# A dense layer's second product written token-major, its outputs rearranged by way of HBM

## The reference

```python
x = x + conv3x3(_gn(x), L0)                  # 8 -> 8 channels, bias
x = x + conv3x3(_gn(x), L1)
x = x + dense(_gn(x))                        # below
x = x + conv3x3(_gn(x), L3)

# dense: one expert e per channel; each image row n is a token of d = 256
h   = einsum('bend,edf->benf', x, w1) + b1   # f = 1024
h   = gelu(h)
out = einsum('benf,efd->bend', h, w2) + b2
```

## Time and profile before

| | |
|---|---|
| median of three runs | 575.45 us |
| the profiled execution | 576.91 us |
| its span | 575.1 us |
| mean granted TensorE clock | 0.971 |
| TensorE busy | 520.0 us, 90% |
| VectorE busy | 374.1 us, 65% |
| ScalarE busy | 291.8 us, 51% |
| GpSimd busy | 159.1 us, 28% |

### The profile page before, as it was taken

How to read it: one execution, slowest core, us unless ns; L and a number is a source line. 1 busy time by engine, 2 the same in 40 slices (tenths; PEclk the granted TensorE clock), 3 DMA queues, 4 the chain that set the end, 5 groups by cost and what they waited for, 6 DMA issues and landing times.

```text
span 575.1 us, 9042 instructions
## 1 busy us (share of the span) xinstructions
PE 520.0 (90%) x3326; PEld 255.5 (44%) x3326; DVE 374.1 (65%) x644; ACT 291.8 (51%) x354; POOL 159.1 (28%) x181
## 2 busy tenths in 40 slices
PE   0879999896979999999999999999999989978990
PEld 0534445364544444444444444444444545445440
DVE  4969999888766395194293392481547598678541
ACT  2599988333635453353362361461444828766510
POOL 4679888853270000000000000000000001677610
PEclk9889999898899999999999999999999999989996
DMA  8845555533020122022011112102123300134769
GB/s 327 324 111 146 150 132 139 143 101 147 0 75 1 73 74 74 0 73 73 0 73 73 31 42 73 73 0 73 74 74 108 112 0 2 45 81 107 242 200 349
DMA packets 14168, 57.41 MB, mean 100 GB/s; under 512 B 3116, under 2 KB 3244, under 8 KB 11052
## 3 DMA queue, kind: packets, MB, share of 16 engines
q1 hardware_dynamic: 11820, 49.30, 26.9%
q10 hardware_dynamic: 2316, 7.68, 3.7%
HBM read 30.03 MB, written 8.39 MB: 67 GB/s over the span
## 4 chain that ended last, share of the span: by engine, by line
PE 62%; DVE 19%; ACT 5%; POOL 4%; DMA 3%; issue 2%; ACTq 1%; SPq 1%; POOLq 0%; DVEq 0%
PE PS L1007 28%; PE PS L978 27%; DVE X L665 6%; DVE ST L626 6%; PE PS L878 2%; POOL XN L360 2%; ACT XN L439 2%; PE PS L952 2%; DMA X<-x 2%; PE PS L936 2%; PE PS L885 1%; DVE X L681 1%; ACT SCR L444 1%; DVE XT L674 1%; DVE SM L641 1%
## 5 line engine op out<-in xcount | busy, mean ns | idle before, releaser
L978 PE MATMUL PS<-XT,W1S 128*128 (+1 forms) x768 | 172.0, 383 | 1.7 <-DVE XT L674 1.7
L1007 PE MATMUL PS<-HID,W2S 128*128 128x512 f16 x768 | 170.8, 379 | 1.6 <-DVE W2S L688 1.6
L476 ACT ACTIVATE SCR<-PS,CONST 128x512 f32<-128x512 f32 x128 | 87.0, 686 | 64.4 <-PE PS L978 27.8
L978 PEld LDWEIGHTS PS<-XT,W1S 128*128 128x128 f16 x768 | 75.6, 99 | 91.1 <-issue 4.7
L1007 PEld LDWEIGHTS PS<-HID,W2S 128*128 128x128 f16 x768 | 75.1, 98 | 87.5 <-issue 1.8
L360 POOL TENSOR_TENSOR XN<-SCR,XN 128x1024 f16<-128x1024 f32 (+1 forms) x61 | 100.4, 1670 | 26.5 <-ACT SCR L444 26.5
L688 DVE SCALAR_TENSOR_TENSOR W2S<-W2F,W2S 128x2048 f16<-128x2048 f32 x10 | 22.9, 2291 | 114.6 <-ACT W2S L472 114.6
L333 POOL MEMSET HALO<- 48x520 f16 x12 | 6.3, 526 | 316.8 <-PE PS L978 316.3
L626 DVE BATCH_NORM_STATS2 ST<-X 128x6 f32<-128x512 f32 x128 | 81.5, 681 | 9.4 <-DMA X<-x 8.2
L439 ACT ACTIVATE XN<-X,SC 128x1024 f16<-128x1024 f32 (+1 forms) x61 | 64.1, 1050 | 33.9 <-POOL SC L351 27.6
L665 DVE SCALAR_TENSOR_TENSOR X<-PS,X 128x512 f32<-128x512 f32 x96 | 59.7, 680 | 21.5 <-PE PS L900 21.5
(11 more groups left out here) (47 smaller groups left out, 442.9 us busy)
## 6 DMA issues: line engine op xcount, KB each, us to landing
W1F<-w SPq DMA_DIRECT2D x10, 1024.0 KB, 4.7
W2F<-w SPq DMA_DIRECT2D x10, 1024.0 KB, 4.8
HALO<-XN SPq DMA_DIRECT2D x48, 129.9 KB
out<-X ACTq DMA_DIRECT2D x12, 512.0 KB, 6.8
HALO<-XN SPq DMA_DIRECT2D x48, 121.8 KB
X<-x SPq DMA_DIRECT2D x2, 2048.0 KB, 19.0
HALO<-XN SPq DMA_DIRECT2D x42, 64.9 KB
HALO<-XN SPq DMA_DIRECT2D x42, 60.9 KB
```

What stands on the lines that cost most here:

```text
L476: act.activation(SCR[:, ft % 2, 0:CH], bank(ft % G_RING), ACT.Gelu, bias=BT[:, ds(e * FT + ft, 1)], scale=1.0 / (XS * WS)).then_inc(gelu_o ...
L978: mm = pe.matmul(bank(ft % G_RING), W1S[:, w, h * NF + ft * P:h * NF + (ft + 1) * P], rhs, start=(n == 0), stop=(n == 3 * DH - 1))
L1007: mm = pe.matmul(bank(G2_BANK + h), W2S[:, w, ft * NW + h * P:ft * NW + (h + 1) * P], HID[slot][:, part, ft], start=(ft == 0 and part == 0 ...
```

## The change

The second product's operands swap places: blocks of 128 tokens of HID are the weights, and W2's high and low part, 256 output features each, are the moving data. A block k of four (two a image, `BLOCKS`) takes, for each hidden tile, one matmul of 512 columns (high tokens x both parts of W2) and one of 256 (low tokens x high part). ScalarE copies the high x low half out of PSUM (`copy_low`), VectorE scales the other half and adds (`evict`), into YT by tokens, or YL for the last part. SP stores each block to `yd` in HBM in X's layout and loads it back into YX. GpSimd adds the bias to X ahead of time and the results of images 0 and 1; VectorE adds those of images 2 and 3. The result transposes are gone. L3 gets seven PSUM banks where it had five; the normal order of steps 8 and 9 on TensorE has no transposes between. The XT layout changes to contiguous tokens.

```diff
+    def store_outputs(e, p, first):
+        for k in range(BLOCKS):
+            sp.wait_ge(yt_ok, first + k + 1)
+            store_tokens(y_tokens(e, p, k), 2 * p + k // NBLK, k % NBLK, e, y_out[p])
...
+        for n, (e, p, load) in enumerate(ENDING[:3]):
+            load_w1(load + 1)
+            load_w2(load + 1)
+            store_outputs(e, p, BLOCKS * (NPAIR * LAST + n))
+            if n == 1:
+                sp.wait_ge(y_out[0], 16 * BLOCKS * NE)
+                for b in range(2):
+                    for k in range(NBLK):
+                        load_outputs(b, k, slice(0, P))
+        sp.wait_ge(y_out[1], 16 * BLOCKS * (NE - 1))
+        sp.wait_ge(g1_mm, NE * NPAIR * FT)
+        for b in range(2, NB):
+            for k in range(NBLK):
+                for w in range(W2):
+                    load_outputs(b, k, slice(w * HALF_P, (w + 1) * HALF_P - R))
+        store_last(0)
...
+        pool.wait_ge(pre_ok, NB * NCH)
+        for b in range(NB):
+            for k in range(NBLK):
...
+                pool.tensor_tensor(half, half, B2.unsqueeze(1).broadcast_to([P, TB, NJ]), ALU.add
+                                   ).then_inc(bias_ok, 1)
...
+                pool.tensor_tensor(xc, y_chunk(b, i), xc, ALU.add).then_inc(y_add, 1)
...
+        def copy_low(to, k, done):
+            act.wait_ge(g2_mm, done)
+            act.activation(to, bank(G2_BANK + k % 2)[:, NW:2 * NW], ACT.Copy,
+                           scale=1.0 / (HS * WS)).then_inc(y_low, 1)
...
+        def add_outputs(i, b):
...
+            dve.tensor_tensor(xc, y_chunk(b, i), xc, ALU.add).then_inc(x_new, 1)
...
+        def evict(to, k, done):
+            dve.wait_ge(y_low, done)
+            dve.scalar_tensor_tensor(out=to, in0=bank(G2_BANK + k % 2)[:, 0:NW],
+                                     scalar=1.0 / (HS * WS), in1=to, op0=ALU.mult, op1=ALU.add
+                                     ).then_inc(yt_ok, 1)
...
-                for part, w in ((0, 0), (1, 0), (0, 1)):
-                    mm = pe.matmul(bank(G2_BANK + h),
-                                   W2S[:, w, ft * NW + h * P:ft * NW + (h + 1) * P],
-                                   HID[slot][:, part, ft],
...
+                pe.matmul(to, HID[slot][:, 0, ft, tokens], both, start=(ft == 0), stop=False)
+                mm = pe.matmul(to[:, 0:NW], HID[slot][:, 1, ft, tokens], high,
+                               start=False, stop=(ft == FT - 1))
```

More of the change, by code:

```diff
@@ L38 @@
 NPAIR = NB // 2
-TT = 2 * NT
+NBLK = 2
+TB = NT // NBLK
+TOK = NBLK * P
+BLOCKS = 2 * NBLK
 XS, WS, HS = 64.0, 256.0, 16.0
@@ L498, in next_w1, with low_block, low_blocks, ending_low @@
             split_high(W1F, W1S, w1_in, w1_hi, e)
[L500 to L508, removed]
-            for p in range(NPAIR):
-                for dh in range(DH):
-                    result(e, p, dh)
+        def copy_low(to, k, done):
+            act.wait_ge(g2_mm, done)
+            act.activation(to, bank(G2_BANK + k % 2)[:, NW:2 * NW], ACT.Copy,
+                           scale=1.0 / (HS * WS)).then_inc(y_low, 1)
+        def low_block(e, p, k):
+            copy_low(y_tokens(e, p, k), k, e * (NPAIR * BLOCKS) + (p * BLOCKS + k + 1))
+        def low_blocks(e):
+            for p in range(NPAIR):
+                for k in range(BLOCKS):
+                    low_block(e, p, k)
+        def ending_low(n, k):
+            e, p, _ = ENDING[n]
+            to = YL[:, k] if n == 3 else y_tokens(e, p, k)
+            copy_low(to, k, BLOCKS * (2 * LAST + n) + k + 1)
         act.wait_ge(cw_in, 16)
@@ L533, in _ @@
         first_hidden()
[L534 to L538, removed]
+        for k, last in enumerate((1, 4, 6, NCH)):
+            for j in range((0, 1, 4, 6)[k], last):
+                xt_high(3 * NCH + j)
+            low_block(0, 0, k)
         hidden(0, 1)
         next_w1(1)
-        result(0, 1, 0)
-        result(0, 1, 1)
+        for k in range(BLOCKS):
+            low_block(0, 1, k)
         def expert(e):
-            act.wait_ge(g2_mm, e * 4)
+            act.wait_ge(g2_mm, e * (NPAIR * BLOCKS))
             split_high(W2F, W2S, w2_in, w2_hi, e)
@@ L611, in _ @@
         store(0)
+        store(1)
         slot_free(11)
@@ L614, in _ @@
             normalise_piece(FIRST_PIECE[11] + k)
-        last_thirds(0)
+        thirds(11, 0)
         normalise_piece(FIRST_PIECE[11] + 4)
-        last_thirds(1)
-        for b in range(1, NB - 1):
-            store(b)
+        thirds(11, 1)
+        store(2)
     @block.vector
@@ L760, in _ @@
         next_w1(1)
+        for k in range(BLOCKS):
+            evict_block(0, 1, k)
         with dve.Fori(1, LAST) as e:
@@ L1022, in expert @@
             for p in range(NPAIR):
-                for h in range(DH):
-                    output(e, p, h)
+                for k in range(BLOCKS):
+                    output(e, p, k)
         pe.wait_ge(cst_in, 16)
@@ L1099, in in_fourth_output @@
                 group_variance(13)
-        between = ((None, None), (None, None), (in_third_hidden, in_third_output),
-                   (in_fourth_hidden, in_fourth_output))
-        for k, (e, p, _) in enumerate(ENDING):
-            hidden(e, p, between[k][0], k)
-            for h in range(DH):
-                output(e, p, h, between[k][1], k)
-        def results(b, first, last):
-            for i in range(first, last + 1):
-                result_transposes(b, i)
-        def last_centres(g, i, n):
-            if n is not None:
-                group_mean(n)
+        for n, (e, p, _) in enumerate(ENDING):
+            hidden(e, p, in_fourth_hidden if n == 3 else None, n)
+            for k in range(BLOCKS):
+                output(e, p, k, in_fourth_output if n == 3 else None, n)
@@ L1116, in last_centres, with four_centres @@
+        def four_centres(g, i):
             for k in range(QUAD):
                 centre(g, i + k)
[L1118 to L1132 removed]
@@ L1133, in _ @@
-        results(3, 6, 7)
-        tiles(9, 0)
-        last_centres(9, QUAD, 15)
-        tiles(9, QUAD)
-        for g in range(10, 12):
-            before_step(g)
-            for i in range(0, NCH, QUAD):
-                last_centres(g, i, None)
-                tiles(g, i)
+        for g in range(8, 12):
+            before_step(g)
+            four_centres(g, 0)
+            tiles(g, 0)
+            four_centres(g, QUAD)
+            if g < 10:
+                group_mean(g + 6)
+            tiles(g, QUAD)
+            if g < 10:
+                group_variance(g + 6)
```

416 lines of the change are left out of this document (219 added, 197 removed).

## The result

The changed kernel takes **628.5 us** (median of 4 runs, 628.4 to 629.42) against 575.86 (574.49 to 577.12) of the kernel before on the same chip: **ratio 1.092, 95% interval 1.089 to 1.095**. Its profiled execution has a span of 626.7 us, 51.6 more than before, and a mean granted clock of 0.929.

| stretch | before, us | after, us | difference | forecast |
|---|---|---|---|---|
| up to the second hidden half of expert 0 | 177.9 | 177.4 | -0.5 | 0 |
| that half and its output | 20.9 | 45.6 | +24.7 | +23 |
| twelve half experts of the loop and parts 0, 1 | 248.7 | 252.5 | +3.9 | +3.7 |
| T to H | 39.6 | 44.5 | +4.9 | +0.8, and 2 for the clock |
| H to the end | 88.1 | 106.7 | +18.6 | +10.7 |

The account below looks back on a forecast made before the run. The prediction took TensorE, busy 90% of the span, with a dense-layer chain of nothing but matmuls, as the bound. Terms 0.6 + 3.1 + 23 + 0.8 + 2 + 10.7 = 40.2 us on 575.45 gave 615 us, range 580 to 636.

Parts of the forecast that it names:

- T to H: From the end of part 1's output (T) to the end of the last hidden tile (H): +0.8 us net.
- H to the end: From the end of the last hidden tile (H) to the end of the span: +10.7 us.
- The second product: Dense layer's second product: same columns in 512 and 256-column matmuls, costing +0.6 us.
- The rival of a 256-column matmul as dear as one of 512: Second product: a 256-column matmul costs as much as its weights and more, +55 us, 670 us; chance 0.03.
- Evictions: Second product's output: TensorE waits for a bank because VectorE evicts only after its W1 split, +3.1 us.
- Bias by GpSimd: Expert 0's second hidden half: GpSimd's eight bias adds hold up VectorE's HID operations, so TensorE stands, +23 us.
- Rival A: Bias adds and tail: GpSimd and VectorE don't hold each other up over long operations, 587 us; chance 0.20.
- Weights behind the results: After part 1's output: part 3's W1 queues behind results, 9.0 us of waiting, net +0.8 us after savings.
- the restart: After two waits of over 8 us TensorE's clock is lower for some microseconds: +2 us, 0 to 5.
- The tail: After the last hidden tile: results' round trip and slower adds delay images 1, 2 and 3, +10.7 us.

Follow-up runs that it names:

- experiment 7: Changed kernel with bias adds moved behind second output blocks of experts 1 to 4, plus VectorE evicting the first output block before its W1 split: 601.93 us.
- experiment 4: Kernel before the change, with eight GpSimd adds of a constant behind the last PRE chunk: 596.86 us against 577.06, ratio 1.035.
- experiment 9: Changed kernel with moved bias adds, plus each half image of images 2 and 3 loaded as 128 rows instead of twice 56: 596.37 us.
- experiments 11: Changed kernel with moved bias adds, part 3's W1 ahead, first evictions before W1 splits, 128-row loads and image 3 loaded later: 593.14 us, ratio 1.028.
- experiment 12: Kernel of experiments 11 with the last expert's fourth block evicted and last two blocks stored before halo copies, image 3 loaded last: 587.68 us, ratio 1.018.

## Why the prediction was right, and where it was off

The median, 628.5, lies 13.5 above the forecast and within the range; the direction and the largest term are as argued. Part by part:

- **The second product: right.** A pair of 512 and 256 columns begins every 325 ns, as forecast. No row of the trace before shows what a matmul of 256 columns costs, so the 0.6 was the author's estimate. In the loop of the changed kernel the pair's 325 ns are 109 more than the 215.8 of a 512-column matmul before, where 1.5 times 215.8 would be 324; that makes 32 pairs 10.40 us against 10.36, and 0.6 in 16 half experts. The rival of a 256-column matmul as dear as one of 512 is out.
- **Evictions: right in size, in part by luck.** Forecast 3.1 and 0.6 for the product, measured 3.9 together. In the loop experiment 7 gives 0.31 us an expert for the order, twice the 0.15 forecast. Parts 0 and 1 lose 1.0 us each, near the 1.1 forecast, but experiment 7 gives only 0.2 of it to the eviction behind the split. The rest is a wait that the prediction has for part 2 alone, with 0.15 us: a block goes through all eight HID tiles in the first 2.6 us of the output, where a half took 5.2, so the last tile is wanted sooner. In part 0 TensorE stands 0.6 us for it; the chain:

```profile
445.44 0.39 PE PS L1124
```

- **Bias by GpSimd: right, shown four ways.** Leaving the adds out, moving them, narrowing them and putting them into the kernel before give 25, 25.6, 10 and 20 us. The term was 23 and came to 24.7. The last HID tile was ready at 213.3 and not at 212.4, because an add takes 4.65 us and not 4.1. The 23 counts both HID operations of a tile as held; for the first, a tensor_scalar with one input in SBUF, no row of the trace before shows a hold, and it was the author's estimate. It took 4.34 to 4.71 us beside the adds (4.39 in experiment 4) and 0.41 after them. Behind it 9.7 us follow, near the forecast 9.3, but not for its reason: the third block doesn't wait for its bank. Instead TensorE's granted clock is 0.50 till 216 us (0.72 on average from 207.4 to 223.0), with pairs every 640 ns for 325, and the second block takes 3.7 us instead of 2.6. The mechanism, one holds and the other waits for the whole instruction, was read from waits of 1.2 us and holds at 4.65. Rival A (587, only bandwidth shared) is out.
- **Weights behind the results: the wait was right, the restart was not.** W1's split begins at T+18.4 (landing forecast at T+18.7), TensorE has its bank back at T+24.8 (T+24.7). The stretch is 4.9 us longer where 0.8 and a share of the 2 stood. Of the difference 2.9 us are the clock: the two blocks after the wait take 8.1 us (500.4 to 508.5) for 5.2. Another 0.9 is in the last hidden tiles (508.5 to 519.75, 11.2 us for 10.4), where TensorE also waits 0.3 us for VectorE's deviation. TensorE's granted clock around that wait:

```profile
487.00:500.00 13.00, 6.38 (x26) 2.63 (x24) 8.94 (x7) 5.07 (x7) 13.00 (x9) 0.85 0.61 255
500.00:506.00 6.00, 5.63 (x18) 2.67 (x19) 3.02 (x6) 0.29 (x1) 6.00 (x6) 0.50 0.17 46
506.00:520.00 14.00, 13.66 (x70) 6.67 (x69) 9.91 (x19) 10.61 (x17) 1.71 (x3) 0.99 0.06 19
```

  For 6 us it runs at 0.50, 3 us of work lost, just when its blocks were the path. I had allowed 2 us for two such places, taken from a row with a wait of 2.8 us; the clock in expert 0 comes on top.
- **The tail: mis-sized, 18.6 for 10.7.** Two of its inputs failed. The 56-row loads were put at the rate of whole rows; they run at half of it (206 against 411 GB/s, experiment 9). And the last two stores were put at H+22, but they queue behind these loads, so that image 1 began at H+34.5 and not H+24.5 (experiments 11, 12). The adds held up by GpSimd's low parts were right: 4.53 and 6.56 us for four, against 2.50 undisturbed, so 2.0 and 4.1 where 2 and 3 stood. With these 5 us the forecast puts image 3 at H+61, and it came 12.9 us later than that. Then 5.0 us came back that nobody forecast: from image 3 to the end it is 32.3 to 32.8 us in every run of the new form, where the prediction kept the old 37.8. So the miss of 7.9 us is smaller than the error of the path. Why the end is shorter stays open. A part of the 12.9 is TensorE's order: the matmuls for image 3's variance stand behind a run of convolution tiles, and from the last statistics to image 3's normalisation it is 8.8 us, where it was 4.9 (7 forecast). In the chain, the sums for mean and variance:

```profile
585.51 0.59 PE PS L981 x2
...
591.37 0.51 PE PS L986 x2
```

So of some 52 us, 25.6 are the place of the bias adds, 6.6 the loads by 56 rows, and 8.7 more the order of queues and evictions (596.4 to 587.7). About 10 us are left (587.68 against 577.6 on the same chip; the remaining 1.7 lie between the two medians of the kernel before, 575.86 and 577.6). What of them is adds from SBUF on VectorE, what the lower clock in the tail (0.84 on average from H to the end in experiment 12, 0.93 before), and what the order of TensorE's steps there, was not separated.

## What to carry to other kernels

An operation on an idle engine is free only if it doesn't hold up another engine's (the eight adds cost 25 us beside the HID operations, and nothing beside the evictions, which stayed at 0.42 us): look at what that engine runs in the same microseconds, and put long GpSimd operations beside VectorE's work from PSUM. Moving data through HBM to save TensorE work that wasn't the end of the chain buys a queue (in the chain here, 13.2 us on W1F<-w and 15.8 on yd<-YL): count who stands behind each copy, stores as well as loads. When a wait is taken away and little comes back, read which instruction of the same engine now stands ahead of the one wanted.

## What the runs showed of the hardware

- A 128x512 tensor_scalar of VectorE with one SBUF input (f32 to f16) was held beside GpSimd's 128x2048 adds, as the two-input operation was: 4.34 us instead of 0.41, and 4.87 instead of 0.69.
- Loads of 56 rows within one half of the rows ran at 206 GB/s, loads of 48 and 8 rows in turn at 176, of 128 rows at 411, all with the copy engines' share at 0.90 or more.
- TensorE was busy for 6.4 of 13 us from 487 to 500. Its granted clock was 0.85 there, then 0.50 from 500 to 506, and 0.99 afterwards.
